# Loading each expert's weights in twelve transfers with rows of 2 KB instead of two with rows of 12 KB

## The reference

```
logits = (x @ wt.T + repeat(g @ wg.T)) / 2              # 8 experts
topk_w, topk_idx = top_k(softmax(logits), 2); topk_w /= topk_w.sum(-1)
gp    = leaky(einsum('th,ehm->etm', x, w_gate))         # h = 512, m = 256
up    = einsum('th,ehm->etm', x, w_up)
y_all = einsum('etm,emh->eth', gp * up, w_down)
y     = sum of the two chosen experts, weighted, + leaky(x @ sw_gate) * (x @ sw_up) @ sw_down
```

## Time and profile before

| what | us |
|---|---|
| median of 3 runs | 1679.45 |
| the 3 runs | 1674.4, 1679.45, 1686.86 |
| the profiled execution, its own time | 1681.98 |
| its span, first to last instruction | 1680.2 |

### The profile page before, as it was taken

The page is one execution under the profiler, slowest core; times in us unless marked ns, Lnnn a source line. Parts: engine busy times, 40 slices in busy tenths (PEclk is TensorE's granted clock), DMA queues, the critical chain, the costliest instruction groups (busy, mean ns, idle before and its releaser), DMA issues. The chain is left out here.

```text
span 1680.2 us, 36541 instructions
## 1 busy us (share of the span) xinstructions
PE 1583.4 (94%) x10236; PEld 1330.0 (79%) x10237; DVE 974.8 (58%) x2954; ACT 714.1 (42%) x1823; POOL 748.5 (45%) x1305
## 2 busy tenths in 40 slices
PE   5899996999999999997999998999999999999999
PEld 4677885998888888896888886878777788778877
DVE  5544525777777777785655556843333343367564
ACT  3232324776777776775322222224333343322221
POOL 1000243786776776875555552342222222155220
PEclk9999998999999999998999998999999999999999
DMA  7576667876776866876557763053465633257431
GB/s 231 197 239 229 219 225 212 236 223 197 226 207 197 238 202 192 238 217 157 201 191 225 230 204 126 1 216 109 175 251 204 253 104 108 86 189 285 153 120 63
DMA packets 181388, 318.12 MB, mean 189 GB/s; under 512 B 17490, under 2 KB 65154, under 8 KB 179220
## 3 DMA queue, kind: packets, MB, share of 16 engines
q1 hardware_dynamic: 150946, 251.59, 46.8%
q0 software_dynamic: 11200, 35.73, 6.9%
q10 hardware_dynamic: 19122, 29.52, 5.1%
HBM read 195.38 MB, written 121.39 MB: 189 GB/s over the span
## 5 line engine op out<-in xcount | busy, mean ns | idle before, releaser
L816 DVE CUSTOM_DVE_ANT_0 scores<-psum,resident 128x514 f32<-128x514 f32 (+3 forms) x512 | 245.6, 489 | 96.1 <-issue 95.9
L890 ACT ACTIVATE probs<-scores,lowest 128x514 f32<-128x514 f32 (+3 forms) x512 | 283.1, 556 | 29.7 <-DVE lowest L816 24.6
L788 POOL TENSOR_SCALAR probs<-probs,rsums 128x512 f32<-128x512 f32 (+3 forms) x512 | 263.1, 524 | 0.0
L937 PE MATMUL psum<-keys,queries 128*128 (+4 forms) x640 | 219.2, 351 | 27.5 <-DMA queries_and_ones<-q_hi_d 17.7
L949 PE MATMUL psum<-ident,probs 128*128 128x128 f32 x1280 | 233.6, 282 | 1.6 <-POOL probs L788 1.2
L937 PE MATMUL psum<-keys_lo_and_mask,queries_and_ones 128*128 (+4 forms) x640 | 183.6, 296 | 0.0
L949 PEld LDWEIGHTS psum<-ident,probs 128*128 128x128 f32 x1280 | 150.2, 141 | 29.5 <-POOL probs L788 20.2
L969 PE MATMUL psum<-probsT,v_now 128*64 128x128 f32 x2560 | 169.4, 279 | 0.9 <-DVE probsT L831 0.9
L937 PEld LDWEIGHTS psum<-keys,queries 128*128 128x128 f32 x640 | 126.3, 197 | 34.6 <-issue 18.5
L969 PEld LDWEIGHTS psum<-probsT,v_now 128*64 128x64 f32 x2560 | 138.5, 138 | 14.5 <-issue 1.8
L899 ACT ACTIVATE probsT<-psum 128x512 f32<-128x512 f32 (+2 forms) x192 | 93.8, 489 | 113.9 <-PE psum L949 97.8
(11 more groups left out here) (244 smaller groups left out, 3698.1 us busy)
## 6 DMA issues: line engine op xcount, KB each, us to landing
ys_d<-y_out ACTq DMA_DIRECT2D x71, 256.0 KB, 2.0
q_hi_d<-q_hi SPq DMA_DIRECT2D x64, 256.0 KB, 2.4
q_lo_d<-q_lo SPq DMA_DIRECT2D x64, 256.0 KB, 2.7
queries<-q_hi_d SPq DMA_DIRECT2D x64, 256.0 KB, 3.7
queries<-q_lo_d SPq DMA_DIRECT2D x64, 256.0 KB, 4.2
queries_and_ones<-q_hi_d SPq DMA_DIRECT2D x64, 256.0 KB, 4.5
oT_d<-o_out SPq DMA_DIRECT2D x64, 256.0 KB, 2.3
o_in<-oT_d SPq DMA_DIRECT2D x32, 512.0 KB, 4.8
```

The lines of the kernel that those rows point to most:

```text
L788: pool.tensor_scalar(out=row, in0=row, scalar1=rsums[:, n % RING:n % RING + 1], scalar2=1.0, op0=ALU.mult, op1=ALU.mult).then_inc(probs_sc ...
L816: dve.tensor_tensor_reduce(out=scores[n % 4][:, 0:CK[i]], in0=score_psum(n), in1=bias_of(resident, i, h), scale=1.0, scalar=3.0e38, op0=AL ...
L890: act.activation(probs[n % RING][:, 0:CK[i]], scores[n % 4][:, 0:CK[i]], ACT.Exp, bias=lowest[:, n % 4:n % 4 + 1], scale=-1.0, accum_out=s ...
L937: last = pe.matmul(whole[:, lo:hi], qs[hp % 2][:, n % 2, i * P:(i + 1) * P], ks[:, bass.ds((b % 2) * (AHEAD + S) + lo, hi - lo)], start=(p ...
```

## The change

Each of the two halves of an expert is fetched in six transfers of 128 rows x 2 KB (DC + MC = 4 + 2 chunks of 512 floats) in place of one of 128 rows x 12 KB. The bytes, their places on chip and the issuing engine stay as they are. The semaphore gets 12 x 16 per load instead of 2 x 16, and the wait in `make_ready` counts accordingly.

```
 def load_expert(eng, dram, experts, e, experts_loaded):
     at = e % PLACES * 2 * EW
     for n, half in enumerate(("w_hi", "w_lo")):
-        eng.dma_start(experts[:, at + n * EW:at + (n + 1) * EW].bitcast(F32), dram[half][e]
-                      ).then_inc(experts_loaded[e % PLACES], 16)
+        for c in range(DC + MC):
+            eng.dma_start(experts[:, at + n * EW + c * D:at + n * EW + (c + 1) * D].bitcast(F32),
+                          dram[half][e][:, c * D:(c + 1) * D]).then_inc(experts_loaded[e % PLACES], 16)
...
-                sp.wait_ge(experts_loaded[e % PLACES], 32 * (e // PLACES + 1))
+                sp.wait_ge(experts_loaded[e % PLACES], 16 * 2 * (DC + MC) * (e // PLACES + 1))
```

## The result

The changed kernel takes 1685.5 us (median of 20 runs) against 1680.43 for the kernel before, a ratio of 1.0026 with a 95% interval of 1.0015 to 1.0036: slower by 4.4 us (2.5 to 6.0); the two medians are 5.1 us apart. The forecast was +8.6 us, 1688, with a range of 1677 to 1700 and 0.83 on a time within 1%. So the range held and the direction was right, but the size lies outside the interval of the measurement: the loss is some 4 us smaller than forecast.

What follows compares the result with a forecast made beforehand. PE, busy 94% of the span, was taken as the bound, losing time where SP's announcements wait behind load issues. Waits of 6.7 us plus 2.0 for the clock made 8.7, so 1688 us against the median of 1679.45; range 1677 to 1700.

Steps and rivals of the forecast that it cites:

- T: Time from the start of a load's first issue to the end of its last: 0.80 us before, 6.0 forecast.
- A: PE's wait for the announcement of expert 3, behind load 4's issue: from 1.26 us to about 6.4.
- B: PE's wait for expert 4, behind load 5's issue: 1.6 us in place of 1.71.
- C: PE's wait for expert 6, behind load 7's issue: 1.6 us where no wait was seen.
- 3T - 11.3: Added waiting at A, B and C together, in us: 6.7 with T = 6.0.
- The landing of load 4: Load 4 should land within a microsecond of 1251, while load 5 is still being issued.
- rival 2: Transfers run one after the other, a load takes 44 us: about 1770 us; chance 0.03.
- Elsewhere: Issues of the other loads, loads 1 and 2 taking some 12 us for 24 issues, cost nothing.
- The clock: PE's clock falls to 1.2 GHz after A, costing 2.0 us; nothing at B and C, upper bound 2.0 each.
- Rival 3: Finer rows free the other queues, so gathers come sooner: no change or faster, 1681 us; chance 0.11.
- Rival 1: The queue fills up and slows SP's issues, T about 11 us: slower by more than 1%, 1706 us; chance 0.11.
- an issue takes 0.7 us or more: Sign that the forecast is wrong, for SP's issues of a load; Rival 1 counts as slower from 0.7 us per issue.

Runs made afterwards that it cites:

- e5: The kernel before with its two transfers of 12 KB rows per load, plus ten transfers of 128 rows x 16 bytes into an unused tile: ratio 1.0162.
- e6: The changed kernel with six transfers of 4 KB rows per load in place of twelve of 2 KB: ratio 0.9981 against the kernel before.
- e4: The changed kernel with load 4 alone put back to two transfers of 12 KB rows: ratio 0.9990 against the kernel before.
- e3: The kernel before, still two issues per load, but with 2 KB rows, the two halves interleaved on chip: ratio 0.9983.

## Why the prediction was right, and where it was off

**The issue time.** Right: 5.6 us plus a stall gave T = 6.0; it was 6.1 to 6.2 at the three places.

**A, B and C.** Right: 6.4, 1.6 and 1.6 us forecast, 6.54, 1.81 and 1.80 measured. The sum 3T - 11.3 gives 7.2 for the three measured T (6.09, 6.21 and 6.21); the waits grew by 7.18. e5 bears the same working out at T of 8.8 to 11.2, e6 at 3.2, and e4 shows that A alone, with the clock behind it, is worth the loss.

**The landing of load 4.** Right: B was set by the issue of load 5 (its end 1252.40, PE's restart 1252.83), not by data. Expert 7's load landed 13.3 us after its first issue (1299.00, announced at 1312.3), no later than the 13.8 of before. The estimate of 31 us for a load, worked out from the fit for transfers from GpSimd in the Trainium skill's "DMA: Bandwidth & Descriptors", section "Anatomy of one DMA — SWDGE (gpsimd) path", laid end to end, is not what these overlapping transfers from SP do: 13.3 us. The same number speaks against rival 2.

**Elsewhere.** Right: loads 1 and 2 took 14.1 us to issue where some 12 were forecast (1107.96 to 1122.05), and no one waited.

**The clock.** Right at A: 0.52 over 4.3 us. At B it fell too, after 1.81 us, where I had put nothing and kept 2.0 as the bound; it cost 1.7. At C, after 1.80 us, it did not fall, nor in e4 after 2.28 and 1.97. The length of the one wait does not decide it. B came some 10 us behind the fall at A, which no other of these waits did; that this is the reason is not shown.

**What the short rows give back.** This step failed. Rival 3 named the mechanism, and I capped it at 0.6 us, because that is PE's listed wait for gathers, and because ACT's 8.4 us for stores "does not reach PE". By the timeline it does, through ACT's rounding of the hidden values and DVE; and for the gathers the weight loads show more than the matmuls (waits of before, 1020 to 1480):

```profile
PEld psum L1882 <- DMA xg<-x_d,slot_rows: 1.4, 3, 0.5
```

The long steps of the kernel before held 3.6 us, and e3 shows 2.9 us (0.2 to 5.7) of gain in time. With that term at 3.6 the sum would have been 8.7 - 3.6 = 5.1 us, inside the measured 2.5 to 6.0. That it meets the difference of the medians to a tenth is luck: the sum holds nothing for the fall of the clock at B. With the profiled execution's own terms it is 10.9 - 3.6 = 7.3, near the 7.6 by which the stage grew without its ends and above the measured interval. Whether the clock falls at B in every execution is not known, so this gap of 1 to 5 us stays open. The two effects do not exclude each other, as the forecast's set of cases had them: issues and rows act in one kernel at once.

**Rival 1.** Something of the kind exists: e3's fourth transfer (4.98 us) and e5's small ones (up to 3.47 us) took far longer to be issued than the others. In the changed kernel one of the 24 issues of loads 1 and 2 took 1.95 us, where nothing waited for it; at the three places that count none took over 0.9 (min/median/max in ns, all loads):

```profile
L169 SPq DMA_DIRECT2D expert_weights<-w_hi_d x48: 327/434/862, 1022.3 to 1301.4; - x48
L169 SPq DMA_DIRECT2D expert_weights<-w_lo_d x48: 428/452/1946, 1025.0 to 1304.8; - x48
```

So the sign "an issue takes 0.7 us or more" holds for single issues and not for their mean of 0.51. What fills up, and at how many rows, these runs do not tell. The sign that gathers land sooner than 6.3 us cannot be read: the profile of the changed kernel lists no landing for them, only that PE no longer waits.

## What to carry to other kernels

Cutting a load into more transfers cost the issuing engine about half a microsecond each here (6.1 us for twelve), and that matters where an announcement, or any other signal, is queued behind them; look for the shortest stretch of work between two loads, not the average one. Long rows can hold up everyone else's transfers, and here the price appeared as late stores and gathers beside a load: compare step lengths inside and outside loads, since a list of waits splits such a delay into pieces too small to see. A middle size (here rows of 4 KB in six transfers, and the one urgent load whole) kept the gain of short rows and took little of the cost of the issues.

## What the runs showed of the hardware

Issues from SP are not of one price: 0.33 us for the first and a median of 0.43 to 0.45 for each further one of 128 rows of 2 KB, 0.54 to 0.65 for 768 rows, but 4.98 for 768 rows behind three such transfers, and up to 3.47 for 128 rows of 16 bytes behind rows of 12 KB. Beside a load of 12 KB rows a gather took 6.3 us (median of three) in place of 3.4, and most stores 8.7 to 10.9 in place of 2.0; beside rows of 4 KB stores took 6.0 to 7.8, and with rows of 2 or 4 KB PE no longer waited for a gather nor ACT for a store. Twelve transfers of 256 KB, issued back to back, landed 13.3 us after the first issue, two of 1.5 MB 13.8. The matrix engine's clock fell after an idle stretch of 1.81 us and stayed after one of 1.80 in the same execution, and after 2.28 in e4; at the ends of the stage it fell in some executions and not in others, which alone moves a stage by up to 2.8 us.
